# Cross-attention and feed-forward block: the second batch's scores and maxima moved from the feed-forward stage into slots 0 to 3 of the softmax stage

## What is computed

```python
n = layernorm(x)
q = (n @ Wq.T)                      # 32 heads of 16
k, v = ctx @ Wk.T, ctx @ Wv.T       # 8 groups of 16, each used by 4 heads
attn = softmax(q k^T / 4)           # 128 x 128 for each head
x = x + (attn v) @ Wfc.T + bfc
m = layernorm(x)
x = x + fp8(gelu(fp8(m) @ Wg0) * (fp8(m) @ Wg1)) @ fp8(Wl)   # hidden 2048
```

## Time and profile before

| | before |
|---|---|
| median of three runs, us | 466.07 (465.42 to 466.16) |
| profiled execution, us | 465.95 |
| span in the profile, us | 463.8 |
| TensorE matmul busy | 430.3 us, 93% |
| TensorE weight load busy | 346.0 us, 75% |
| VectorE busy | 334.6 us, 72% |
| ScalarE busy | 313.0 us, 67% |
| GpSimd busy | 236.4 us, 51% |
| mean granted clock of TensorE | 0.978 |

### The profile page before, as it was taken

The page is one execution under the profiler, slowest core; times in us unless marked ns, Lnnn a source line. Parts: engine busy times, 40 slices in busy tenths (PEclk is TensorE's granted clock), DMA queues, the critical chain, the costliest instruction groups (busy, mean ns, idle before and its releaser), DMA issues.

```text
span 463.8 us, 11802 instructions
## 1 busy us (share of the span) xinstructions
PE 430.3 (93%) x4620; PEld 346.0 (75%) x4620; DVE 334.6 (72%) x704; ACT 313.0 (67%) x578; POOL 236.4 (51%) x226
## 2 busy tenths in 40 slices
PE   7867969889999999999999999999999999899997
PEld 6746848767787877877787878877787878558973
DVE  4776587976897579966897579966897579575542
ACT  6848784987379745977379745977379744885541
POOL 5577982695228713684228813684228812492000
PEclk9967799999999999999999999999999999999999
DMA  7797769264602560045401551035401251000001
GB/s 286 283 255 287 230 182 294 79 206 133 161 3 56 152 136 28 3 98 152 116 4 37 152 142 39 3 94 156 118 3 42 76 126 37 3 24 24 3 25 45
DMA packets 21239, 49.79 MB, mean 107 GB/s; under 512 B 4672, under 2 KB 5184, under 8 KB 21184
## 3 DMA queue, kind: packets, MB, share of 16 engines
q1 hardware_dynamic: 20862, 48.24, 36.2%
q10 hardware_dynamic: 322, 0.80, 0.7%
HBM read 23.86 MB, written 4.19 MB: 60 GB/s over the span
## 4 chain that ended last, share of the span: by engine, by line
PE 62%; DVE 11%; issue 8%; POOL 8%; ACT 7%; DMA 2%; ACTq 1%; POOLq 0%; SPq 0%; DVEq 0%
PE bank L644 16%; PE bank L664 10%; PE bank L443 6%; PE bank L445 6%; PE bank L444 6%; PE bank L551 5%; POOL plo L1297 5%; PE bank L518 4%; DVE mneg L1081 4%; PE bank L478 3%; PE bank L569 2%; PE bank L571 2%; ACT phi L840 1%; DMA qs<-cq 1%; DVE prod L1146 1%
## 5 line engine op out<-in xcount | busy, mean ns | idle before, releaser
L1297 POOL TENSOR_TENSOR plo<-p,phi 128x512 f16<-128x512 f32 x128 | 149.8, 1181 | 60.9 <-ACT phi L840 59.9
L644 PE MATMUL bank<-x2T,wgate 128*128 128x128 fp8e4 x2048 | 131.3, 221 | 3.6 <-DVE xr L1159 3.2
L644 PEld LDWEIGHTS bank<-x2T,wgate 128*128 128x128 fp8e4 x2048 | 117.0, 99 | 19.2 <-issue 12.1
L837 ACT ACTIVATE p<-bank 128x512 f32<-128x512 f32 x128 | 77.6, 606 | 20.0 <-PE bank L551 19.6
L1081 DVE TENSOR_REDUCE mneg<-bank 128x4 fp32r<-128x512 f32 x128 | 84.4, 684 | 7.6 <-PE bank L518 7.2
L840 ACT ACTIVATE phi<-bank 128x512 f16<-128x512 f32 x128 | 77.4, 605 | 0.0
L664 PE MATMUL bank<-wlin,act 128*128 128x512 fp8e4 x256 | 72.4, 378 | 0.0
L859 ACT ACTIVATE gate<-bank 128x512 bf16<-128x512 f32 x64 | 38.2, 597 | 50.1 <-PE bank L644 37.3
L863 ACT CAST ff<-bank 128x512 bf16<-128x512 f32 x64 | 37.5, 587 | 49.3 <-PE bank L644 49.3
L518 PE MATMUL bank<-kmask,cq 128*128 128x512 f32 x128 | 58.1, 480 | 4.5 <-DVE mneg L1081 2.8
L551 PE MATMUL bank<-qs,ks 98*128 98x512 f32 x128 | 55.5, 434 | 5.1 <-ACT phi L840 2.5
(11 more groups left out here) (117 smaller groups left out, 813.2 us busy)
## 6 DMA issues: line engine op xcount, KB each, us to landing
qs<-cq SPq DMA_DIRECT2D x90, 128.0 KB, 2.5
stage<-in_w SPq DMA_DIRECT2D x14, 512.0 KB, 5.4
ks<-khl SPq DMA_DIRECT2D x96, 64.0 KB, 2.0
cin<-in_ctx SPq DMA_DIRECT2D x8, 512.0 KB, 4.4
xr<-in_x SPq DMA_DIRECT2D x16, 256.0 KB, 4.5
out<-xr SPq DMA_DIRECT2D x16, 256.0 KB, 2.7
xr<-in_w SPq DMA_DIRECT2D x6, 512.0 KB, 6.2
raw_g<-in_w SPq DMA_DIRECT2D x4, 512.0 KB, 5.9
```

The source lines that it names most:

```text
L644: mm = pe.matmul(out[:, h * SEQ:(h + 1) * SEQ], wgate8[:, UH * v + h, kk, part, :], x2T[:, b % NB, kk, :], start=kk == 0, stop=kk == KT - 1)
L837: act.activation(p32[:, e % P32BUF, :], T[n % 2][:, :], ACT.Exp, scale=QUARTER).then_inc(p32_ok, 1)
L1297: pool.tensor_tensor(plo[:, e % PBUF, :], p32[:, e % P32BUF, :], phi[:, e % PBUF, :], ALU.subtract).then_inc(plo_ok, 1)
```

## The change

It changes where work lies, not what is computed.

- The eight scores and maxima of a pair's second batch leave the feed-forward stage of the pair before. They lie in slots 0 to 3 of the pair's own softmax stage, two to a slot, on VectorE first in the slot.
- `turn_max` of the second batch moves from slot 3 to 5; the next pair's K from slots 0, 1 to 4, 5, V from 2, 3 to 6, 7, X from 5, 6 to 8, 9, Q from 8 to 15 to 11 to 18. In stage 0 they stay where they are. With the new order of the list V follows K on one bank.
- Three early scores instead of four in slots 16 to 18; the others of the first batch in units 0 to 3: 3 in unit 0, 4 in unit 1 behind `project_out`, 5 and 6 in unit 2, 7 in unit 3. On VectorE the first maximum of a unit stands ahead of the product, and so of `residual` in unit 1.
- The statistics for x of the next pair (`norm_stats`, and `norm_rstd` on GpSimd) move from slot 0 to unit 5 of the stage before, from pair 3 on.

```diff
@@ -64,12 +64,17 @@
 
 SLOTS = TILES + LAG + 1
 
-S_MAX = 3
-S_K, S_V, S_X = (0, 1), (2, 3), (5, 6)
-S_Q = {True: tuple(range(7, 15)), False: tuple(range(8, 16))}
-M_UNIT, M_UNIT_0 = 5 / 8, 2
-S_EARLY = {16: 1, 17: 1, 18: 2}
+S_MAX = {True: 3, False: 5}
+S_K = {True: (0, 1), False: (4, 5)}
+S_V = {True: (2, 3), False: (6, 7)}
+S_X = {True: (5, 6), False: (8, 9)}
+S_Q = {True: tuple(range(7, 15)), False: tuple(range(11, 19))}
+S_SECOND = 4
+S_EARLY = {True: {16: 1, 17: 1, 18: 2}, False: {16: 1, 17: 1, 18: 1}}
+S_UNIT = {True: {0: (4, 5), 1: (6, 7)}, False: {0: (3,), 1: (4,), 2: (5, 6), 3: (7,)}}
+M_UNIT = {True: 2, False: 5}
 M_EARLY = {17: 1, 18: 1}
+N_UNIT = 5
 EARLY_BANK = ("T0", "T1")
 EVEN_TURN = 15
 S_NORM = 0
@@ -114,12 +119,14 @@
     keys = []
     for p in range(NP):
         q = p + 1
+        if p:
+            keys += [("S", p, 1, s) for s in range(SBANKS)]
         if q < NP:
-            keys += [("K", q), ("V", q)]
-        keys += [("M", p, 1)]
-        if q < NP:
+            keys += [("K", q), ("M", p, 1), ("V", q)] if p else [("K", q), ("V", q), ("M", p, 1)]
             keys += [("X", q, 0), ("X", q, 1), ("Q", q, 0), ("Q", q, 1)]
-            keys += [("S", q, i, s) for i in range(NB) for s in range(SBANKS) if not early_bank(q, i, s)]
+            keys += [("S", q, 0, s) for s in range(SBANKS) if not early_bank(q, 0, s)]
+        else:
+            keys += [("M", p, 1)]
     seq += [(key, f"A{n % 2}") for n, key in enumerate(keys)]
     at, last, in_front = {}, {}, {}
     for key, name in seq:
@@ -667,18 +674,19 @@
 
             def prepare(q, n):
 
+                first = q == 1
                 for half in range(2):
-                    if n == S_K[half]:
+                    if n == S_K[first][half]:
                         project_k(q, 2 * half, 2 * half + 2)
                 for b in range(NB):
-                    if n == S_V[b]:
+                    if n == S_V[first][b]:
                         project_v(q, b)
                 for i in range(NB):
-                    if n == S_X[i]:
+                    if n == S_X[first][i]:
                         turn_x(q, i)
                 for j in range(HPG):
                     for half in range(2):
-                        if n == S_Q[q == 1][2 * j + half]:
+                        if n == S_Q[first][2 * j + half]:
                             project_q(q, j, 2 * half, 2 * half + 2)
 
             warm_up()
@@ -705,6 +713,11 @@
                 for n in range(SLOTS):
                     if n < TILES:
                         scores_t(p, n)
+                    if p and n < S_SECOND:
+                        for s in (2 * n, 2 * n + 1):
+                            scores(p, 1, s)
+                    if n == S_MAX[first] and p:
+                        turn_max(p, 1)
                     if n == chain["turn"]:
                         turn_out(c_b)
                     if p and n == EVEN_TURN:
@@ -716,7 +729,7 @@
                             down(b, 2 * (n - at), 2 * (n - at) + 2)
                     if q < NP:
                         prepare(q, n)
-                    if n == S_MAX:
+                    if n == S_MAX[first] and first:
                         turn_max(p, 1)
                     for k in range(KT):
                         if n == chain["project"][k]:
@@ -724,31 +737,29 @@
                     if n == (chain["turn2"] if q < NP else LAST_TURN2):
                         turn_x2(c_b)
                     if q < NP:
-                        for s in range(early, early + S_EARLY.get(n, 0)):
+                        for s in range(early, early + S_EARLY[first].get(n, 0)):
                             scores(q, 0, s)
-                        early += S_EARLY.get(n, 0)
+                        early += S_EARLY[first].get(n, 0)
                 ups = len(up_batches(p)) * UPB
                 c_b = NB * p
-                per = TILES // ups if q < NP else 0
                 for k in range(ups):
+                    late = S_UNIT[first].get(k, ()) if q < NP else ()
                     if p == NP - 1 and k == 4:
                         turn_out(c_b + 1)
-                    if p and q < NP and k == int(M_UNIT * ups):
+                    if p and q < NP and k == M_UNIT[first]:
                         turn_max(q, 0)
                     up(p, k, 0)
                     if p and k == 1:
                         project_out(c_b, 0, KT)
                     if p and k == 3:
                         turn_x2(c_b)
-                    for s in range(per * k, per * k + per):
-                        if s % per == per // 2:
-                            up(p, k, 1)
-                        if s >= early:
-                            scores(q, *divmod(s, SBANKS))
-                    if first and k == M_UNIT_0:
+                    for s in late[:1]:
+                        scores(q, 0, s)
+                    up(p, k, 1)
+                    for s in late[1:]:
+                        scores(q, 0, s)
+                    if first and k == M_UNIT[first]:
                         turn_max(q, 0)
-                    if not per:
-                        up(p, k, 1)
                     if p == NP - 1:
                         if k == 4:
                             project_out(c_b + 1, 0, KT)
@@ -940,7 +951,7 @@
                 for n in range(SLOTS):
                     if n < TILES:
                         weights(p, n)
-                    if n == S_MAX:
+                    if n == S_MAX[first]:
                         max_rows(p, 1)
                     if first and n == SLOTS - 2:
                         select_rows(1)
@@ -953,16 +964,16 @@
                     if n == (chain["turn2"] if q < NP else LAST_TURN2):
                         x2_out(c_b)
                     if q < NP:
-                        if n == S_K[1]:
+                        if n == S_K[first][1]:
                             keys_hi(q)
-                        if n == S_V[1]:
+                        if n == S_V[first][1]:
                             values_half(q)
-                        if n == S_V[1] + 1:
+                        if n == S_V[first][1] + 1:
                             values_hi(q)
                         for i in range(NB):
-                            if n == S_X[i]:
+                            if n == S_X[first][i]:
                                 xT_high(q, i)
-                        if n == S_V[1] + 3:
+                        if n == S_V[first][1] + 3:
                             values_mid(q)
                         for h in range(2):
                             if n == S_Q[first][4 * h + 3]:
@@ -1192,6 +1203,9 @@
                 early = 0
                 for n in range(SLOTS + 1):
                     m, odd = divmod(n - LAG - 1, 2)
+                    if p and n < S_SECOND:
+                        for s in (2 * n, 2 * n + 1):
+                            maxima(p, 1, s)
                     if q < NP and n < SLOTS:
                         for s in range(early, early + M_EARLY.get(n, 0)):
                             maxima(q, 0, s)
@@ -1211,18 +1225,18 @@
                         roots_2(c_b)
                         norm2_apply_psum(c_b)
                     if q < NP:
-                        if n == S_NORM:
+                        if n == S_NORM and p < 2:
                             norm_stats(q)
-                        if n == S_K[1] + 1:
+                        if n == S_K[first][1] + 1:
                             keys_lo(q)
-                        if n == S_V[1]:
+                        if n == S_V[first][1]:
                             values_sum(q)
                         if n == S_NORM + 1:
                             roots_1(q)
                         for i in range(NB):
                             if n == S_NORM + 2:
                                 norm_apply_psum(q, i)
-                            if n == S_X[i] + 1:
+                            if n == S_X[first][i] + 1:
                                 xT_low(q, i)
                         for h in range(2):
                             if n == S_Q[first][4 * h + 3] + 1:
@@ -1233,25 +1247,24 @@
                         chunk(late.pop(0))
                 ups = len(up_batches(p)) * UPB
                 u0, c_b = UPB * up_batches(p)[0], NB * p
-                per = TILES // ups if q < NP else 0
                 for k in range(ups):
+                    late_s = S_UNIT[first].get(k, ()) if q < NP else ()
                     if q < NP and k == 0:
-                        for s in range(early, sum(S_EARLY.values())):
+                        for s in range(early, sum(S_EARLY[first].values())):
                             maxima(q, 0, s)
-                        early = sum(S_EARLY.values())
                     if p and k == 2:
                         norm2_apply(c_b)
                     if p == NP - 1 and k == 5:
                         out_lo(c_b + 1)
-                    for s in range(per * k, per * k + per):
```

(21 more changed lines are left out.)

## The result

The changed kernel takes **510.93 us** (median of four runs, 510.04 to 512.45), the kernel before 466.12 in the same comparison (465.42 to 468.26): ratio 1.0956, 95% interval 1.0909 to 1.1004. The prediction said slower, and the time lies in its range of 479 to 512; it is 9.9 above the forecast of 501. Of the rise of 44.8 us the forecast had 35. The waits stand where it had put them, but those of slots 0 to 3 and the one behind `queries_lo` are longer, and the late preparation alone costs more than the walk had said.

What follows compares the result with a forecast made beforehand. TensorE's matmul queue at its own pace was taken as the bound, VectorE close behind. Five steady pairs at +5.6 (+28), pair 1 +7, stage 0 -1.5, last pair +1.8 sum to +35.3: 501 us, range 479 to 512.

Steps and rivals of the forecast that it cites:

- slots 0 to 3, K at slot 4: Softmax stage: scores on two banks in turn, then the K group, wait for VectorE's maxima; +1.9 us a pair.
- V on keys_lo: Softmax stage: V takes K's bank and so waits for keys_lo; +0.4 us a pair.
- Q at slot 11: Softmax stage: Q waits for both xT_low, behind values_sum, residual and norm work on VectorE; +2.3 us a pair.
- score on queries_lo: Unit 0: the score takes the second Q group's bank and waits for queries_lo; +0.4 us a pair.
- turn_x2 on norm2: Feed-forward stage: score 4's maximum, product and act_fp8 precede residual in unit 1, so turn_x2 waits; +1.5 us a pair.
- unit 4 on x2T: Feed-forward stage: later product, gate copy and x2_out make x2T late for TensorE; +0.7 us a pair.
- old waits gone: TensorE's two waits for VectorE in a steady pair disappear; 0.5 + 0.5 us less a pair.
- Pair 1, +7: Pair 1: norm_stats of pair 2 and chunk conversions stand among the maxima and ahead of xT_low; +7 us.
- rival C: New waits at Q and slots 0 to 3 make TensorE's granted clock fall six times; +10, 511 us; 18%.
- likeliest case: The whole kernel: the forecast itself, 501 us, with 494 to 508 for this case alone; 48%.
- Rival A: Balance: TensorE stays bound by its pace and late stages follow; about -13, 453 us; 9%.
- Rival B: Half the waits: those of slots 0 to 3 and Q partly hidden; +3 us a pair, 484 us; 20%.

Runs made afterwards that it cites:

- chain_late: The changed kernel with the odd batch's residual and norm2 behind the second xT_low (residual at slot 11, not 8) and turn_x2 at slot 14: 509.29 us.
- resid_first: The changed kernel with no score in unit 1 (4 and 5 in unit 2, 6 and 7 in unit 3), so residual follows the projection: 502.95 us.
- combo2_banks: The changed kernel without unit 1's score, statistics in unit 1, odd residual chain behind xT_low, turn_out at slot 16, three second-batch scores in O0 and O1: 492.92 us.
- norm_unit1: The changed kernel with the next pair's norm_stats in unit 1 of the feed-forward stage instead of unit 5: 509.0 us.
- prep_late: The changed kernel with the second batch's scores and maxima back beside the units and norm_stats in slot 0; K, V, X, Q stay late: 504.91 us.
- clock_kept: The changed kernel with 18 transposes, whose result nobody reads, ahead of the first T matmul of pair 1: 512.73 us.
- only_last: The kernel before with the second batch's scores and maxima moved in the last pair alone, three in O0 and O1, turn_max at slot 5: 464.54 us, ratio 0.9955.
- spread: The kernel of combo2_banks with the odd batch's four output projection groups in slots 5, 8, 9 and 10 instead of 4 to 7: 488.39 us.

## Why the prediction was right, and where it fell short

**Right:** the sign, against what a balance of loads would say, and its ground: a queue of TensorE without slack, with an order on VectorE close behind it. The prediction counted its waits by where TensorE would want to start, so the estimate by starts in the section on the result is what to hold against them. In us a steady pair:

| step | forecast | by starts | idle in the rows |
|---|---|---|---|
| slots 0 to 3, K at slot 4 | 1.9 | 3.1 | 1.5 |
| V on keys_lo | 0.4 | 0.6 | 0.3 |
| Q at slot 11 | 2.3 | 1.9, and 0.4 at the T | 1.2 |
| score on queries_lo | 0.4 | 1.1 | 0.9 |
| turn_x2 on norm2 | 1.5 | 1.6 | 1.4 |
| unit 4 on x2T | 0.7 | 0.7 | 0.6 |
| old waits gone | -1.0 | -1.3 | -1.0 |
| cheaper scores, and small delays that went | -0.6 | -1.2 | |
| pair | +5.6 | +6.9 | |

- *Q at slot 11:* the place, the chain and the size were right, instruction by instruction, in this timeline of VectorE. With the chain out of the way (chain_late) the step T11 to T12 is 1.3 shorter.

```profile
221.59 0.42 DVE L1072 TENSOR_TENSOR vsum<-bank,vhalf 128x256 f32<-128x256 f32 x1 [3.51 <-ACT vhalf L810]
221.93 0.28 DVE L1115 TENSOR_TENSOR ao<-osum,bank 128x128 f32<-128x128 f32 x1
222.12 0.68 DVE L1170 TENSOR_TENSOR xr<-xr,bank 128x512 f32<-128x512 f32 x1
222.72 0.68 DVE L1129 TENSOR_TENSOR xr<-xr,bank 128x512 f32<-128x512 f32 x1
...
225.16 0.68 DVE L1007 TENSOR_TENSOR cx<-bank,cx 128x512 fp32r<-128x512 f32 x1
...
226.15 0.75 DVE L1151 SCALAR_TENSOR_TENSOR xn<-xr,mv,bank 128x512 fp8e4<-128x512 f32 x1
226.81 0.68 DVE L1007 TENSOR_TENSOR cx<-bank,cx 128x512 fp32r<-128x512 f32 x1
```

- *turn_x2 and x2T:* right in size, but resid_first took out 1.35 a pair, not 2.2: the freed time is partly lost again at the next maxima.
- *The feed-forward stage stays at 22:* 22.7.

**Where it failed:** the step "a pair +5.6", which measured 6.9, and in it two terms.

- *Slots 0 to 3, +1.9 against 3.1.* The mechanism is there, and combo2_banks, with two banks more and VectorE on time, has T4 1.3 sooner. But the walk had VectorE free for the first maximum at 1.7 us, and it starts there at 2.5 (205.57, counted from 203.06). Two things were left out. `norm_stats` in unit 5 was **costed at nothing**: moved to unit 1 it gives back 0.6 (norm_unit1). And a product in front of it takes 1.51 us instead of 0.41 (202.89, last section); no run shows its share apart. The sum had also lost the 0.13 of the K group: its own terms come to 2.0.
- *queries_lo, +0.4 against 1.1.* It stood on VectorE behind the first maximum and a sum as well (240.81, with the first maximum at 239.50), which the walk had left out.

The walk also never priced slots 0 to 3 without K and V, where ScalarE takes about 2.5 of TensorE's time when nothing else stands there (prep_late). In the changed kernel maxima hold these slots instead. So moving the preparation alone costs 5.6 where the prediction's terms for it give 2.6 (2.3 + 0.4 + 0.4 less 0.5), and adding the scores and maxima to that costs 1.4 more, where it had 3.0. That the two parts together came near the measured pair is partly luck.

**Pair 1, +7 against +10.4,** is the second miss. The fall of the clock that rival C warned of came there and in no later pair: granted clock 0.64 over 80 to 92, so 1.2 GHz for much of it, where the kernel before had 1.00 (2.4 GHz), and 1.00 in all of 144 to 506 (first fences). At 0.82 over 28 us the clock withheld some 5 us of full speed, at most what the fall cost. The Trainium skill, "TensorE: Matmul & The Clock Gate", Part 1, has the idle state as the throttled one. The fall agrees with that in kind, but waits of up to 1.4 in every later pair brought none in this kernel, and filling half of the wait ahead of it did not stop it (clock_kept).

The time lies in the range, but above the 494 to 508 of the likeliest case, in the part that the range owes to rival C, which had the clock fall six times. It fell in pair 1 alone. So the pairs being dearer fill a part of the range that stood for something else, and that it was wide enough is partly luck.

Rival A (453) fell by every run; the Trainium skill, "Perfetto Trace Analysis", section Optimization Strategy, has it that interleaving such regimes may help, and that holds here only for the last pair, where TensorE did have idle time (only_last). Rival B (484, half the waits) fell too: a pair is 6.9 longer, not 3, with a wait at each step.

What stays open: which of the delays left between spread and the kernel before (3 us a pair, 2.9 of them by the starts) could still be removed; how much of pair 1's length is the clock's and how much its DMA's; and what brings the clock's fall.

## What to carry to other kernels

When work is moved out of a place, price the hole as well as the new place: here K and V had covered ScalarE's table load and exponentials, and with nothing in their place TensorE lost about 2.5 us a pair (prep_late), before the first of the eight maxima was put there. Count a wait by the starts of instructions, not by the idle time in the row: here the idle in the rows had grown by 4.9 of 6.9 us. Before moving a vector instruction "to where the engine has room", look whether its queue is waiting there or behind: the same 2.15 us of statistics cost 0.6 more a pair in unit 5 than in unit 1 (norm_unit1). And make such a move first in the one stage whose trace shows idle time; there it paid.

## What the runs showed of the hardware

A bf16 product on VectorE, or its cast to fp8, takes 0.41 to 0.43 us, and up to 1.5 when it starts beside GpSimd's 128x512 f32 tensor_tensor on the context. Rows of VectorE and of GpSimd, first in the changed kernel:

```profile
202.10 0.41 DVE L1157 TENSOR_TENSOR prod<-gate,ff 128x512 bf16<-128x512 bf16 x1
...
202.89 1.51 DVE L1157 TENSOR_TENSOR prod<-gate,ff 128x512 bf16<-128x512 bf16 x1
...
202.68 1.44 POOL L1294 TENSOR_TENSOR cx<-cin,cx 128x512 fp32r<-128x512 f32 x1 [0.52 <-ACT cx L794]
```

In norm_unit1 it hits the cast:

```profile
262.85 1.52 DVE L1164 TENSOR_SCALAR act<-prod 128x512 fp8e4<-128x512 bf16 x1
...
262.81 1.28 POOL L1294 TENSOR_TENSOR cx<-cin,cx 128x512 fp32r<-128x512 f32 x1 [0.27 <-ACT cx L794]
```

And in the kernel before, where the product starts near GpSimd's end:

```profile
187.57 0.64 DVE L1146 TENSOR_TENSOR prod<-gate,ff 128x512 bf16<-128x512 bf16 x1
...
186.66 1.27 POOL L1281 TENSOR_TENSOR cx<-cin,cx 128x512 fp32r<-128x512 f32 x1 [1.12 <-ACT cx L783]
```

All three end 0.28 behind GpSimd's instruction (204.40 and 204.12, 264.37 and 264.09, 188.21 and 187.93): so it looks as if VectorE's was held until GpSimd's was done, and not slowed. In the kernel before, 16 of the 128 products and casts take over 0.5 us, each beside such an instruction of GpSimd (on the context, or on x with its bias), and none of the 112 others does. In the changed kernel six casts start up to 0.2 us ahead of GpSimd's instruction, and none of them is longer. The Trainium skill, "SBUF — State Buffer", section "SBUF: two separate sides", has the two engines share a pair of ports as an exclusive lock, and these rows agree. One such instruction a pair (1.51 instead of 0.41) adds up to 1.1 us to the backlog with which VectorE enters slots 0 to 3; whoever moves VectorE's queue in time moves what it meets on GpSimd.
